# Two routers of a transformer kernel: position tables in 16 bits with the tile innermost, code products from written-out 16-bit tables

## The chip, the cores and the metric

The kernel runs on one core of one Trainium2 chip. The metric is the device time of one launch in microseconds (us). Five engines work side by side from queues of their own: PE (TensorE, matrix products; PEld is its loading of weights), DVE (VectorE), ACT (ScalarE), POOL (GpSimd) and SP (SyncE, which here only issues DMA).

## The reference, cut to what matters

2048 tokens of 256 numbers pass through two layers. Each layer has a mixing part (attention in layer 0) and then a layer of eight experts that a router chooses. Only the routers are touched here:

```python
# layer 0: the best expert of each token, at most C = 320 tokens per expert
top1 = jnp.argmax(logits, axis=-1)
mask = jax.nn.one_hot(top1, E, dtype=jnp.int32)
ranks = jnp.cumsum(mask, axis=0) - 1
mask = mask * (ranks < C).astype(jnp.int32)
...
dispatch = jnp.einsum('tec,th->ech', sec_mask, tokens)
# layer 1: the two best experts of each token, no limit
vals, idx = jax.lax.top_k(scores, TOP_K)
...
coef = (jax.nn.one_hot(sel, gate_w.shape[0], dtype=x.dtype) * mult[..., None]).sum(axis=1)
out = jnp.einsum('te,eth->th', coef, y)
```

## The kernel before

The 2048 tokens are 16 tiles (NT) of 128 (P), one token of a tile on each partition. The program is a row of phases, each a block of five instruction streams, one per engine. A barrier of all engines ends each block; its place in the profile is the branch line behind the phase (L983 behind router 0, L1436 behind router 1). The phases are `phase_front` (attention of layer 0), `phase_router0`, `phase_experts0`, `phase_mix`, `phase_router1`, `phase_experts1`. Within a stream the order is that of the code; engines wait for each other by semaphores.

Both routers do the same. PE turns the normalized rows, multiplies by the gate and turns the logits back. DVE, one small step after another, finds the best expert of each token, the rank of the token within its expert, and from it a slot: a block number and a position in the block of 0 to 127. Then the map token to slot has to be turned round into slot to token:

- `at_blk` (L1210, L1646) is 1 where the token's block is b. NS0 = 24 blocks in router 0; NB = 39 blocks and two choices j per token in router 1.
- `code` or `code_of` is `at_blk` times the number of the partition, plus one (`tok1`, L1211, L1649), and `at_blk` times the number of the tile (`iota_hi`, L1212, L1650).
- `at_pos` (L1215, two halves of 8 tiles; L1653, one instruction for each choice) is 1 where the token's position is p: every position p of a token is compared with the numbers 0 to 127 in `iota_pos`.
- PE multiplies `at_pos` of a tile, as weights, with the tile's codes and sums over the tiles (L1099, L1541). The sum at (p, b) is the token in slot p of block b.

DVE reads it out (`tok0`, L1234; `tok_of`, L1664), and POOL gathers the rows of the first blocks from DRAM by an indirect DMA (L974, L944) as the last thing of the block. In `phase_experts1`, `at_pos` of router 1 is used once more, on 32 weight loads, to carry the weights of the tokens to their slots (L2257, shown as e_w). In router 0 SP issues bulk loads all the time (weights of expert 1, and those of the mixing part, L952 and L960).

The number tables are written by POOL at the start of each router's block, one `iota` after another (`numbers`, L1252 and L1669), in 32-bit floats: router 0 has eight and DVE waits for them at its `wait_ge(iota_ready, 8)`; router 1 has seven and DVE waits for six of them. At that time DVE runs the start of its own stream: `memset` and copy of `gT` (L1592, L1593 in router 1), `normal_rows` (L140: 128x256 each, four for a quarter of the tokens), and then `turned` (L1147, L1582), half of the copy of the turned rows, on which PE's product of logits waits (L1051, L1492).

Two helpers set the shape of an operand:

```python
def bcast(ap, n):        # [p, w] read as [p, n, w]: the whole row again and again
    return ap.unsqueeze(1).to_broadcast([ap.shape[0], n, ap.shape[1]])
def last_bcast(ap, n):   # [p, w] read as [p, w, n]: each element n times in a row
    return ap.unsqueeze(2).to_broadcast([ap.shape[0], ap.shape[1], n])
```

Of the kernel before, what the change touches and what calls it, by code (L numbers as in the profile page):

```python
# [978 lines left out]
def phase_router0(nc, k, a, sem):  # L979
# [3 lines left out]
    with ctx:  # L983
        def sb(name, shape, dt=FP):
            return ctx.enter_context(nc.sbuf_tensor("r0_" + name, shape, dt))
# [13 lines left out]
        logits, best, diff = sb("logits", [P, NT, E]), sb("best", [P, NT]), sb("diff", [P, NT, E])  # L999
        desc, iota_pos, iota_b = sb("desc", [P, E]), sb("iota_pos", [P, P]), sb("iota_b", [P, NS0])  # L1000
        iota_hi, iota_empty, tok1 = sb("iota_hi", [P, NT]), sb("iota_empty", [P, E, NST]), sb("tok1", [P, 1])
        upper = sb("upper", [P, 1])
# [3 lines left out]
        tot, run, rank = sb("tot", [P, E, NT]), sb("run", [P, E, NT]), sb("rank", [P, NT, E])  # L1006
        sel, hi2, pos, blk = sb("sel", [P, NT]), sb("hi2", [P, NT]), sb("pos", [P, NT]), sb("blk", [P, NT])
        full, sel_i = sb("full", [P, NT]), sb("sel_i", [P, NT], mybir.dt.int32)
        at_pos, at_blk = sb("at_pos", [P, NT, P], BF), sb("at_blk", [P, NT, NS0], BF)
        code = sb("code", [P, NT, 5, NS0], BF)  # L1010
# [33 lines left out]
        def _(pe):  # L1044
# [53 lines left out]
            def invert(out, c0, c1, i):  # L1098
                return nc.tensor.matmul(out, at_pos[:, i, :], code[:, i, c0:c1, :].rearrange("p c b -> p (c b)"),  # L1099
                                        start=(i == 0), stop=(i == NT - 1))  # L1100
# [39 lines left out]
        def _(dve):  # L1140
# [70 lines left out]
            step(ts(code[:, :, 0, :], at_blk[:, :, :], tok1[:, 0:1], None, ALU.mult))  # L1211
            step(tt(code[:, :, 1, :], at_blk[:, :, :], last_bcast(iota_hi[:, :], NS0), ALU.mult))  # L1212
            for half in range(2):
                some = slice(NT // 2 * half, NT // 2 * (half + 1))
                tt(at_pos[:, some, :], bcast(iota_pos[:, :], NT // 2), last_bcast(pos[:, some], P),  # L1215
                   ALU.is_equal).then_inc(pos_ready, 1)
# [32 lines left out]
        @block.gpsimd  # L1249
        def _(pool):  # L1250
            def numbers(out, pattern, base, each):
                nc.gpsimd.iota(out, pattern=pattern, base=base, channel_multiplier=each,  # L1252
                               allow_small_or_imprecise_dtypes=True).then_inc(iota_ready, 1)

            numbers(desc[:, :], [[-1, E]], E, 0)
            numbers(iota_b[:, :], [[1, NS0]], 0, 0)
            numbers(iota_pos[:, :], [[1, P]], 0, 0)
            numbers(iota_hi[:, :], [[1, NT]], 0, 0)
            numbers(tok1[:, :], [[0, 1]], 1, 1)
            for r in range(NST - 1):  # L1260
# [172 lines left out]
def phase_router1(nc, k, a, sem):  # L1433

    ctx = ExitStack()
    with ctx:  # L1436
# [15 lines left out]
        best, pri, rest = sb("best", [P, NT]), sb("pri", [P, NT, E]), sb("rest", [P, NT, E])  # L1452
        desc, iota_b, iota_pos = sb("desc", [P, E]), sb("iota_b", [P, NB]), sb("iota_pos", [P, BLK])
        iota_end, iota_hi, tok1 = sb("iota_end", [P, NB]), sb("iota_hi", [P, 2 * NT]), sb("tok1", [P, 1])
        cont, chosen = sb("cont", [P, E, NT]), sb("chosen", [P, NT, E], BF)
# [3 lines left out]
        pick, slot = sb("pick", [P, 2, NT, E]), sb("slot", [P, 2 * NT])  # L1459
        slot_i, blk_of, pos = sb("slot_i", [P, 2 * NT], mybir.dt.int32), sb("blk_of", [P, 2 * NT]), sb("pos", [P, 2 * NT])  # L1460
        code_of = sb("code_of", [P, 2, NT, 2, NB], BF)
        cmp_b, blk_e = sb("cmp_b", [P, NB, E]), sb("blk_e", [P, NB])
        inv = sb("inv", [P, NB])
# [21 lines left out]
        def _(pe):  # L1485
# [52 lines left out]
            for j in range(2):  # L1538
                pe.wait_ge(pos_ready[j], 1)
                for i in range(NT):  # L1540
                    last = nc.tensor.matmul(pinv[:, 0:2 * NB], k.at_pos[:, j, i, :],  # L1541
                                            code_of[:, j, i, :, :].rearrange("p s b -> p (s b)"),
                                            start=(j == 0 and i == 0), stop=(j == 1 and i == NT - 1))
# [31 lines left out]
        def _(dve):  # L1575
# [62 lines left out]
            for j in range(2):  # L1638
# [10 lines left out]
            step(ts(code_of[:, :, :, 0, :].rearrange(flat4), at_blk[:, :, :, :].rearrange(flat4), tok1[:, 0:1], None, ALU.mult))  # L1649
            tt(code_of[:, :, :, 1, :].rearrange(flat4), at_blk[:, :, :, :].rearrange(flat4), last_bcast(iota_hi[:, :], NB),  # L1650
               ALU.mult).then_inc(code_ready, 1)
            for j in range(2):
                tt(k.at_pos[:, j, :, :], bcast(iota_pos[:, :], NT), last_bcast(pos[:, NT * j:NT * (j + 1)], BLK),  # L1653
                   ALU.is_equal).then_inc(pos_ready[j], 1)
# [11 lines left out]
        @block.gpsimd  # L1666
        def _(pool):
            def numbers(out, pattern, base, each):
                nc.gpsimd.iota(out, pattern=pattern, base=base, channel_multiplier=each,  # L1669
                               allow_small_or_imprecise_dtypes=True).then_inc(iota_ready, 1)  # L1670

            numbers(desc[:, :], [[-1, E]], E, 0)
            numbers(iota_b[:, :], [[1, NB]], 0, 0)
            numbers(iota_pos[:, :], [[1, BLK]], 0, 0)
            numbers(iota_end[:, :], [[BLK, NB]], 0, 0)
            numbers(iota_hi[:, :].rearrange("p (j i) -> p j i", j=2), [[0, 2], [1, NT]], 0, 0)
            numbers(tok1[:, :], [[0, 1]], 1, 1)
# [479 lines left out]
def phase_experts1(nc, k, a, sem, out):  # L2157
# [4 lines left out]
    with ctx:  # L2162
# [43 lines left out]
        def _(pe):  # L2206
# [46 lines left out]
            def slot_weights():  # L2253
                pe.wait_ge(wcode_ready, 1)
                for n in range(2 * NT):
                    j, i = divmod(n, NT)
                    last = nc.tensor.matmul(pw[:, :, :].rearrange("p n b -> p (n b)"), k.at_pos[:, j, i, :],  # L2257
                                            k.wcode[:, j, i, :, :].rearrange("p n b -> p (n b)"),
                                            start=(n == 0), stop=(n == 2 * NT - 1))
                last.then_inc(w_done, 1)  # L2260
# [337 lines left out]
```

## Time and profile before

| | us |
|---|---|
| median of 3 runs | 1077.09 (1077.02 to 1078.98) |
| the profiled execution | 1082.88 |
| its span in the profile | 1081.2 |
| PE busy | 965.0 (89%) |
| DVE busy | 634.9 (59%) |
| ACT busy | 525.2 (49%) |
| POOL busy | 291.7 (27%) |

The profile is that of one execution, 1082.88 us long; instructions and waits are read from its span of 1081.2 us. Router 0 lies from 507.4 to 546.0 us of it, the experts of layer 0 up to 710, the mixing part up to 803.4, router 1 from 803.4 to 839.8, the experts of layer 1 behind it. The profile names a buffer by its first letters and without numbers (`r_at_pos`, `r_code`; both routers' are `r_...`; `k_at_pos` is that of router 1; `r_plT` and `e_w` are banks of PSUM; `k_hT` at L2363 is the table of weight codes). A line number is that of the kernel printed above.

### The profile page before, as it was taken

To read this page: it belongs to the slowest core of one execution; us is meant where nothing else is said; L and a number is where in the kernel's file an instruction comes from. 1 tells how busy PE (TensorE), PEld (TensorE's weight loads), DVE (VectorE), ACT (ScalarE), POOL (GpSimd) and SP (SyncE) were. 2 spreads that over 40 slices of the span, in tenths; PEclk is the share of its full clock that TensorE was granted. 3 is DMA by queue.
4 is the path that set the end of the run, shared out by engine and by line. 5 is a ranking of instruction groups with operands and counts; after the bars stand their busy time and mean duration, and the time that the engine had idled before them with its cause. 6 is when DMAs were issued, how large, how long until landed. Compare 5 with 4: busy or idle time off the path is not lost. (4 is left out here: it accounts for less than half of the span.)

```text
span 1081.2 us, 24756 instructions
## 1 busy us (share of the span) xinstructions
PE 965.0 (89%) x9947; PEld 635.2 (59%) x9951; DVE 634.9 (59%) x1667; ACT 525.2 (49%) x825; POOL 291.7 (27%) x345
## 2 busy tenths in 40 slices
PE   7788899999999999997579999967885899999993
PEld 4333335444444444444257777755664799999993
DVE  5568999999898979675610000088677533333331
ACT  3432567777875786763222213176443444444440
POOL 2100420110111111132024342225450155544541
PEclk9978999999999999998879999989997899999997
DMA  5880000000000000011935668230560033332224
GB/s 188 171 181 15 2 2 2 3 3 2 3 3 2 3 2 2 2 4 64 371 103 146 215 178 269 44 85 1 176 214 1 25 53 51 47 49 49 47 41 96
DMA packets 63279, 78.87 MB, mean 73 GB/s; under 512 B 12096, under 2 KB 54976, under 8 KB 62736
## 3 DMA queue, kind: packets, MB, share of 16 engines
q1 hardware_dynamic: 50688, 61.54, 19.0%
q0 software_dynamic: 11968, 15.47, 8.6%
q8 instruction: 68, 1.11, 0.4%
q10 hardware_dynamic: 528, 0.52, 0.1%
q14 instruction: 27, 0.22, 0.1%
HBM read 58.12 MB, written 21.36 MB: 74 GB/s over the span
## 5 line engine op out<-in xcount | busy, mean ns | idle before, releaser
L622 ACT ACTIVATE k_prob<-f_s 128x1024 f32<-128x1024 f32 (+3 forms) x320 | 270.1, 896 | 121.5 <-PE f_s L460 120.9
L682 DVE TENSOR_REDUCE k_mpart<-f_r 128x1 f32<-128x512 f32 x384 | 250.5, 685 | 34.5 <-PE f_r L403 32.2
L403 PE MATMUL f_r<-k_ks,k_qs 112*32 112x512 bf16 (+3 forms) x2560 | 211.8, 357 | 20.7 <-DMA k_qs<-q_dram 8.1
L460 PE MATMUL f_s<-k_qs,k_ks 114*32 114x512 bf16 (+3 forms) x2560 | 174.9, 350 | 1.9 <-ACT k_prob L622 1.3
L882 POOL TENSOR_SCALAR_AFFINE_SELECT k_prob<-k_prob 128x256 f32<-128x256 f32 x128 | 51.2, 406 | 383.9 <-ACT k_prob L622 382.7
L403 PEld LDWEIGHTS f_r<-k_ks,k_qs 112*32 112x32 bf16 x2560 | 70.1, 95 | 137.4 <-DVE k_mpart L682 56.7
L476 PE MATMUL f_o<-k_prob,k_vaug 128*32 128x512 f32 (+3 forms) x1280 | 146.6, 531 | 1.5 <-POOL k_prob L882 1.4
L679 DVE CUSTOM_DVE_ANT_0 k_unread<-f_r,k_causal 128x128 bf16<-128x128 f32 (+3 forms) x256 | 121.0, 484 | 18.7 <-PE f_r L403 17.7
L460 PEld LDWEIGHTS f_s<-k_qs,k_ks 114*32 114x32 bf16 x2560 | 65.3, 97 | 78.5 <-issue 27.5
L2321 DVE TENSOR_TENSOR mid<-silu_g,e_u 128x512 f32<-128x512 f32 x39 | 26.8, 688 | 112.7 <-PE e_u L2222 111.7
L1406 DVE SCALAR_TENSOR_TENSOR outr<-p_o,k_w,k_mod 128x256 f32<-128x256 f32 x16 | 7.7, 484 | 131.1 <-PE p_o L1347 131.1
L2222 PE MATMUL e_g<-xT,k_rot_t 128*128 128x128 f32 x624 | 77.9, 279 | 2.9 <-ACT xT L147 2.9
L2222 PEld LDWEIGHTS e_g<-xT,k_rot_t 128*128 128x128 f32 x624 | 77.2, 195 | 5.4 <-ACT xT L147 3.5
L2409 POOL DMA_INDIRECT sum<-y,k_row_of x39 | 62.3, 1598 | 65.1 <-DVE y L2332 51.8
L1378 ACT ACTIVATE mid<-p_h 128x320 f32<-128x320 f32 x64 | 28.0, 437 | 104.1 <-PE p_h L1335 104.1
L2222 PE MATMUL e_u<-xT,k_rot_t 128*128 128x128 f32 x624 | 77.1, 277 | 0.0
L1335 PE MATMUL p_h<-rowsT,k_w1T 128*128 128x320 f32 x256 | 73.8, 448 | 1.2 <-ACT rowsT L147 1.2
L2222 PEld LDWEIGHTS e_u<-xT,k_rot_t 128*128 128x128 f32 x624 | 74.0, 195 | 0.0
L2233 PE MATMUL e_y<-k_w1T,mid 128*128 x312 | 73.6, 379 | 0.0
L944 POOL DMA_INDIRECT k_xb<-h_rows,k_tok_of x39 | 44.8, 1148 | 91.9 <-PE e_x L2216 54.5
L1424 POOL DMA_INDIRECT sum<-outr,k_row x24 | 37.8, 1576 | 93.4 <-DVE outr L1406 91.6
L1335 PEld LDWEIGHTS p_h<-rowsT,k_w1T 128*128 128x128 f32 x256 | 49.6, 196 | 22.8 <-issue 3.2
(403 smaller groups left out, 1264.9 us busy)
## 6 DMA issues: line engine op xcount, KB each, us to landing
k_w1T<-in_L_ffn_w_dram SPq DMA_DIRECT2D x18, 512.0 KB, 9.8
k_w1T<-in_L_ffn_wi_dram SPq DMA_DIRECT2D x8, 1024.0 KB, 5.9
k_w1T<-in_L_ffn_wo_dram SPq DMA_DIRECT2D x8, 1024.0 KB, 9.4
k_qs<-q_dram SPq DMA_DIRECT2D x6, 768.0 KB, 9.4
h_rows<-k_h SPq DMA_DIRECT2D x8, 512.0 KB, 6.6
sum<-k_x SPq DMA_DIRECT2D x8, 512.0 KB, 6.7
q_dram<-k_room SPq DMA_DIRECT2D x12, 256.0 KB, 9.2
k_rot_t<-in_L_ffn_w_dram SPq DMA_DIRECT2D x6, 512.0 KB, 4.9
```

The source lines that it names most:

```text
L403: last = nc.tensor.matmul(dst[32 * j:32 * (j + 1), :], qs[0:KROWS, c, GH * g + hs, q0:q0 + 32], ks[0:KROWS, QC * ck:QC * ck + w], start=Tr ...
L460: last = nc.tensor.matmul(sc[h % 2][32 * j:32 * (j + 1), i, off:QC], ks[0:KALL, k0:k0 + 32], qs[0:KALL, c, GH * g + 2 * pair + i, off:QC], ...
L476: last = nc.tensor.matmul(ot[32 * j:32 * (j + 1), off:QC], vaug[:, kt, :], prob[:, u % 2, j, off:QC], start=(kt == 0), stop=(kt == TQ * (c ...
L622: nc.scalar.activation(prob[:, u % 2, 2 * pair:2 * pair + 2, off:QC], sc[h % 2][:, :, off:QC], ACT.Exp, scale=HD ** -0.5).then_inc(e_done, 1)
L679: nc.vector.tensor_tensor_reduce(unread[:, r % RING, 0:w], bank(r)[:, 0:w], causal[:, QC - w:QC], 1.0, NEG, ALU.add, ALU.max, mpart[:, s % ...
L682: nc.vector.reduce_max(mpart[:, s % 2, hs, t, ck:ck + 1], bank(r)[:, 0:w], AX.X).then_inc(ring_used[r % RING], 1)
L882: nc.gpsimd.affine_select(out=block_, in_=block_, compare_op=ALU.is_ge, fill=0.0, base=0, pattern=[[0, 2], [1, P]], channel_multiplier=-1) ...
L944: nc.gpsimd.indirect_dma_start(out=k.xb[:, b % 2, :], out_offset=None, in_=k.h_rows, in_offset=bass.IndirectOffsetOnAxis(ap=k.tok_of[:, b: ...
L1335: last = nc.tensor.matmul(ph[n % 2][:, 0:CAP], wi[:, s, t, P * n:P * (n + 1)], rowsT[:, s, t, :], start=(t == 0), stop=(t == KH - 1))
L2222: last = nc.tensor.matmul(out[:, P * c:P * (c + 1)], w[:, s, F1 * t + P * c:F1 * t + P * (c + 1)], xT[:, s, t, :], start=(t == 0), stop=(t ...
L2233: last = nc.tensor.matmul(py[s][:, :], m[:, s, P * c:P * (c + 1)], k.w1T[:, e, 2, D * c:D * (c + 1)], start=(c == 0), stop=(c == FT - 1))
L2409: nc.gpsimd.indirect_dma_start(out=k.sum1, out_offset=bass.IndirectOffsetOnAxis(ap=k.row_of[:, b:b + 1], axis=0), in_=y[:, s, :], in_offse ...
```

## The change

Three things change in each router, and nothing in the order of any stream: each engine has as many instructions as before, in the same order.

- `at_pos` is stored as (position, tile) in place of (tile, position), so that the 16 tiles of a position are next to each other. It is computed from a table `all_pos` of the same shape, which holds the position 16 times over, and from `pos`, both in 16 bits. `pos` is now read as a row of 8 or 16 elements again and again.
- The product with the tile's number takes a table `hi_of` in the full shape of `at_blk`, in 16 bits, in place of `iota_hi`. The codes keep their layout.
- PE reads `at_pos` of a tile as weights with a step of 16 elements (32 bytes) between columns, in place of a step of one: 32 weight loads in router 0, 32 in router 1 and 32 in the experts of layer 1.

POOL writes the two tables: in router 0, 2048 elements in place of 128 and 384 in place of 16; in router 1, 2048 in place of 128 and 1248 in place of 32; all in 16 bits in place of 32.

```diff
# phase_router0
+        all_pos, hi_of = sb("all_pos", [P, P, NT], BF), sb("hi_of", [P, NT, NS0], BF)
...
-                return nc.tensor.matmul(out, at_pos[:, i, :], code[:, i, c0:c1, :].rearrange("p c b -> p (c b)"),
+                return nc.tensor.matmul(out, at_pos[:, :, i], code[:, i, c0:c1, :].rearrange("p c b -> p (c b)"),
...
-            step(tt(code[:, :, 1, :], at_blk[:, :, :], last_bcast(iota_hi[:, :], NS0), ALU.mult))
+            step(tt(code[:, :, 1, :], at_blk[:, :, :], hi_of[:, :, :], ALU.mult))
...
-                tt(at_pos[:, some, :], bcast(iota_pos[:, :], NT // 2), last_bcast(pos[:, some], P),
+                tt(at_pos[:, :, some], all_pos[:, :, some], bcast(pos[:, some], P),
                    ALU.is_equal).then_inc(pos_ready, 1)
...
-            numbers(iota_pos[:, :], [[1, P]], 0, 0)
-            numbers(iota_hi[:, :], [[1, NT]], 0, 0)
+            numbers(all_pos[:, :, :], [[1, P], [0, NT]], 0, 0)
+            numbers(hi_of[:, :, :], [[1, NT], [0, NS0]], 0, 0)
# phase_router1
-                    last = nc.tensor.matmul(pinv[:, 0:2 * NB], k.at_pos[:, j, i, :],
+                    last = nc.tensor.matmul(pinv[:, 0:2 * NB], k.at_pos[:, j, :, i],
...
-            tt(code_of[:, :, :, 1, :].rearrange(flat4), at_blk[:, :, :, :].rearrange(flat4), last_bcast(iota_hi[:, :], NB),
+            tt(code_of[:, :, :, 1, :].rearrange(flat4), at_blk[:, :, :, :].rearrange(flat4), hi_of[:, :, :],
                ALU.mult).then_inc(code_ready, 1)
...
-                tt(k.at_pos[:, j, :, :], bcast(iota_pos[:, :], NT), last_bcast(pos[:, NT * j:NT * (j + 1)], BLK),
+                tt(k.at_pos[:, j, :, :], all_pos[:, :, :], bcast(pos[:, NT * j:NT * (j + 1)], BLK),
                    ALU.is_equal).then_inc(pos_ready[j], 1)
...
-            numbers(iota_pos[:, :], [[1, BLK]], 0, 0)
+            numbers(all_pos[:, :, :], [[1, BLK], [0, NT]], 0, 0)
             numbers(iota_end[:, :], [[BLK, NB]], 0, 0)
-            numbers(iota_hi[:, :].rearrange("p (j i) -> p j i", j=2), [[0, 2], [1, NT]], 0, 0)
+            numbers(hi_of[:, :, :].rearrange("p (j i) b -> p j i b", j=2), [[0, 2], [1, NT], [0, NB]], 0, 0)
# phase_experts1
-                    last = nc.tensor.matmul(pw[:, :, :].rearrange("p n b -> p (n b)"), k.at_pos[:, j, i, :],
+                    last = nc.tensor.matmul(pw[:, :, :].rearrange("p n b -> p (n b)"), k.at_pos[:, j, :, i],
```

## Rows read from the trace of the kernel before

**Rows 1.** The chain that ended last, shares of the span by line.

```profile
by line: PE e_g L2222 6.7%; PE e_u L2222 6.5%; PE e_y L2233 6.1%; PE e_x L2216 0.8%; DMA sum<-y,k_row_of 0.3%; PE e_w L2257 0.2%; issue 0.2%; POOL sum L2409 0.1%; ACT xT L147 0.1%; ACTq L2291 0.1%; DVE y L2332 0.0%; ACT k_rot_t L2292 0.0%; 
```

**Rows 2.** DVE late in router 0, in order of time (start, duration, in us).

```profile
531.05 2.36 DVE L1215 TENSOR_TENSOR r_at_pos<-r_iota_pos,r_pos 128x1024 bf16<-128x1024 f32 x2
533.94 1.50 DVE L1221 TENSOR_TENSOR r_code<-r_at_blk,r_w_part 128x384 bf16<-128x384 bf16 x3
536.27 0.18 DVE L1234 CAST k_tok<-r_row 128x24 uint32<-128x24 f32 x1
```

**Rows 3.** Router 0's end on POOL, SP and PE, and its gathers' time to landing.

```profile
540.18 0.91 POOL L974 DMA_INDIRECT k_rows<-h_rows,k_tok  x1 [0.30 <-issue]
DMA to landing us min/median/max: 5.4/5.4/6.1
542.57 0.90 SPq L960 DMA_DIRECT2D k_bq<-in_L_attn_b_in_dram  x1
546.05 1.87 PE L1323 MATMUL p_t<-k_ident,k_rows 128*128 128x128 f32 x6 [9.41 <-PEq L983]
```

**Rows 4.** DVE at the end of router 1.

```profile
829.27 4.49 DVE L1653 TENSOR_TENSOR k_at_pos<-r_iota_pos,r_pos 128x2048 bf16<-128x2048 f32 x2
835.14 0.20 DVE L1662 COPY r_inv<-r_plT 128x39 f32<-128x39 f32 x1
835.60 0.18 DVE L1664 TENSOR_SCALAR k_tok_of<-k_slot 128x39 uint32<-128x39 f32 x1
```

**Rows 5.** Router 1's end on PE and POOL; a stretch: busy by engine, granted clock 0.78.

```profile
833.81 1.22 PE L1541 MATMUL r_plT<-r_code_of,k_at_pos 128*128 128x78 bf16 x16 [0.91 <-DVE k_at_pos L1653]
836.64 1.07 POOL L944 DMA_INDIRECT k_xb<-h_rows,k_tok_of  x1 [32.23 <-DVE k_tok_of L1664]
831.00:831.50 0.50, 0.00 (x0) 0.00 (x0) 0.50 (x2) 0.00 (x0) 0.00 (x0) 0.78 0.00 0
```

**Rows 6.** DVE groups by line and shape (busy us, mean ns of one).

```profile
L2363 DVE TENSOR_TENSOR k_hT<-k_at_blk,e_w_hi 128x1248 bf16<-128x1248 bf16 x3 | 4.2, 1454 | 0.0
L1649 DVE TENSOR_SCALAR r_code_of<-k_at_blk,r_tok 128x1248 bf16<-128x1248 bf16 x1 | 0.6, 553 | 0.0
```

**Rows 7.** The start of router 1 on POOL, DVE and PE.

```profile
803.68 0.29 DVE L1593 COPY r_gT<-k_g_in 128x16 f32<-128x16 f32 x1
803.70 0.23 POOL L1669 IOTA r_iota_pos<- 128x128 f32 x1
805.11 0.80 DVE L1582 TENSOR_SCALAR k_hT<-r_tp,k_modcol_b 128x512 f32<-128x512 f32 x1
806.62 1.41 PE L1492 MATMUL r_plT<-k_hT,r_gT 128*32 128x512 f32 x4
```

**Rows 8.** The start of router 0, and the same copy of gT without POOL beside it.

```profile
507.62 1.40 DVE L140 TENSOR_SCALAR k_h<-k_x,k_mv,k_rstd 128x256 f32<-128x256 f32 x4
509.07 3.25 PE L178 MATMUL r_tp<-k_ident,k_h 128*128 128x128 f32 x14 [0.57 <-DVE k_h L140]
510.30 0.16 DVE L1164 COPY r_gT<-k_g_in 128x16 f32<-128x16 f32 x1
```

**Rows 9.** POOL and DVE side by side in the attention; all runs of L663.

```profile
479.04 0.41 POOL L882 TENSOR_SCALAR_AFFINE_SELECT k_prob<-k_prob 128x256 f32<-128x256 f32 x1 [0.51 <-ACT k_prob L622]
479.15 0.44 DVE L663 TENSOR_SCALAR k_gate_sgn<-k_mod 128x256 f32<-128x256 f32 x1
L663 DVE TENSOR_SCALAR k_gate_sgn<-k_mod x2: 289/364/440, 116.7 to 479.1; 128x256 f32<-128x256 f32 x2
```

**Rows 10.** POOL: a short iota in time, and a 16-bit output by line and shape.

```profile
803.47 0.14 POOL L1669 IOTA r_desc<- 128x8 f32 x1 [0.52 <-POOLq L1689]
L831 POOL TENSOR_SCALAR k_minus<-k_ident 128x128 bf16<-128x128 f32 x1 | 0.6, 585 | 0.4 <-DMA k_bo<-in_L_attn_bo_dram 0.4
```

**Rows 11.** Part of the longest chain in the experts of layer 1, in order of time.

```profile
856.00 1.78 PE e_g L2222 x16
861.52 1.73 PE e_w L2257 x32
```

More of the change, by code:

```diff
@@ L999, in phase_router0 @@
         logits, best, diff = sb("logits", [P, NT, E]), sb("best", [P, NT]), sb("diff", [P, NT, E])
-        desc, iota_pos, iota_b = sb("desc", [P, E]), sb("iota_pos", [P, P]), sb("iota_b", [P, NS0])
-        iota_hi, iota_empty, tok1 = sb("iota_hi", [P, NT]), sb("iota_empty", [P, E, NST]), sb("tok1", [P, 1])
+        desc, iota_b = sb("desc", [P, E]), sb("iota_b", [P, NS0])
+        iota_empty, tok1 = sb("iota_empty", [P, E, NST]), sb("tok1", [P, 1])
         upper = sb("upper", [P, 1])
@@ L1006, in phase_router0 @@
         tot, run, rank = sb("tot", [P, E, NT]), sb("run", [P, E, NT]), sb("rank", [P, NT, E])
-        sel, hi2, pos, blk = sb("sel", [P, NT]), sb("hi2", [P, NT]), sb("pos", [P, NT]), sb("blk", [P, NT])
+        sel, hi2, pos, blk = sb("sel", [P, NT]), sb("hi2", [P, NT]), sb("pos", [P, NT], BF), sb("blk", [P, NT])
         full, sel_i = sb("full", [P, NT]), sb("sel_i", [P, NT], mybir.dt.int32)
-        at_pos, at_blk = sb("at_pos", [P, NT, P], BF), sb("at_blk", [P, NT, NS0], BF)
+        at_pos, at_blk = sb("at_pos", [P, P, NT], BF), sb("at_blk", [P, NT, NS0], BF)
+        all_pos, hi_of = sb("all_pos", [P, P, NT], BF), sb("hi_of", [P, NT, NS0], BF)
         code = sb("code", [P, NT, 5, NS0], BF)
@@ L1452, in phase_router1 @@
         best, pri, rest = sb("best", [P, NT]), sb("pri", [P, NT, E]), sb("rest", [P, NT, E])
-        desc, iota_b, iota_pos = sb("desc", [P, E]), sb("iota_b", [P, NB]), sb("iota_pos", [P, BLK])
-        iota_end, iota_hi, tok1 = sb("iota_end", [P, NB]), sb("iota_hi", [P, 2 * NT]), sb("tok1", [P, 1])
+        desc, iota_b = sb("desc", [P, E]), sb("iota_b", [P, NB])
+        iota_end, tok1 = sb("iota_end", [P, NB]), sb("tok1", [P, 1])
         cont, chosen = sb("cont", [P, E, NT]), sb("chosen", [P, NT, E], BF)
@@ L1459, in phase_router1 @@
         pick, slot = sb("pick", [P, 2, NT, E]), sb("slot", [P, 2 * NT])
-        slot_i, blk_of, pos = sb("slot_i", [P, 2 * NT], mybir.dt.int32), sb("blk_of", [P, 2 * NT]), sb("pos", [P, 2 * NT])
+        slot_i, blk_of, pos = sb("slot_i", [P, 2 * NT], mybir.dt.int32), sb("blk_of", [P, 2 * NT]), sb("pos", [P, 2 * NT], BF)
         code_of = sb("code_of", [P, 2, NT, 2, NB], BF)
+        all_pos, hi_of = sb("all_pos", [P, BLK, NT], BF), sb("hi_of", [P, 2 * NT, NB], BF)
         cmp_b, blk_e = sb("cmp_b", [P, NB, E]), sb("blk_e", [P, NB])
@@ L2536, in build @@
         with experts1:
-            k.at_pos = sbuf(experts1, "at_pos", [P, 2, NT, BLK], BF)
+            k.at_pos = sbuf(experts1, "at_pos", [P, 2, BLK, NT], BF)
             k.hT1 = sbuf(experts1, "hT1", [P, 2 * KH * QC])
```

## The prediction

> **What bounds the kernel now.** I read the longest chain first: it ends in the experts of layer 1, in PE's products back to back [rows 1]. Then the two routers in order of time, engine by engine: there nobody is busy throughout, and PE and POOL wait for DVE's small steps. So a router's end is set by one chain, and what that gains or loses moves everything behind it.
>
> Router 0 [rows 2, 3]: DVE works without a pause up to `k_tok`, written at 536.45; then POOL gathers, the third gather starts at 540.18 and lands 5.4 us later, at about 545.6; PE goes on at 546.05 behind the barrier. SP's last issue ends at 543.47, so the gathers end last and SP some 2 us ahead of them. Router 1 [rows 4, 5]: DVE writes `k_tok_of` at 835.78, POOL gathers from 836.64, and the block ends. Just before, two things meet: PE's last product ends at 835.03, and DVE, busy until then, reads it at 835.14. At the start of both routers DVE's L140 leads to PE's next step: in router 0 PE waits for it (0.57 us), in router 1 `turned` (805.11 to 805.91) is done 0.7 us before PE can start the logits at 806.62 [rows 7, 8].
>
> **Part 1: DVE's tables.** Price of a two-input operation: 1.18 us for 1024 elements (2.36 for two) [rows 2], 2.25 for 2048 (4.49 for two) [rows 4]: 1.04 ns an element and 0.11 us fixed. Two 16-bit inputs alone don't help: L2363 has them, one repeated along the innermost dimension, and takes 1454 ns for 1248, the full price. A one-input operation on as many 16-bit elements takes 553 ns [rows 6], so 16-bit elements can be taken several at a time. For a two-input one the trace has no such row. Bounds: nothing gained, and half the elements' time. I take the half, since now every operand is 16-bit with neighbours next to each other. Then each operation loses half its elements' time.
>
> - Router 0: two halves of `at_pos`, each 0.53 less; code product, 192 elements' time of 384, 0.20 less. Sum 1.26.
> - Router 1: two `at_pos`, each 1024 x 1.04, 1.06 less; code product, 624 elements' time of 1248 (priced by L2363, its like), 0.65 less. Sum 2.77.
>
> The Trainium skill ("VectorE: DVE Perf Modes", What auto-detection actually checks) says that a two-input operation runs two elements a cycle if every tensor is 16-bit with step one. By it the sums are these; without it they would be zero. No row here shows it.
>
> All of this is on the chain, if PE keeps up. In router 1 the first `at_pos` is ready at about 829.8 in place of 831.5, PE needs for 16 pairs of load and product 1.22 us even at the low clock [rows 5], the second is ready at 831.0, so PE ends by 832.3, when DVE is ready to read too (835.1 - 2.77). In router 0 PE has the three code products of L1221 as cover (1.50 us). The clock falls from 2.4 to 1.2 GHz about 831.3 (0.78 granted over 831.0 to 831.5, [rows 5]), so the first 16 pairs run no slower than now.
>
> **Part 2: PE's weight loads, step 32 bytes.** Now a pair takes 76 ns in router 1 (1.22 by 16, low clock) and 54 ns in the experts (1.73 by 32) [rows 5, 11], with products of 78 and 117 columns, so a load hides behind a product. No weight load of this kernel has a step now. Lower bound: no change. Upper bound, by the slowest row of pairs: a 32-bit load and product, 111 ns (1.78 by 16) [rows 11], and 222 at half the clock. That would cost 32 x 0.057 = 1.8 us at L2257, and in router 1: 13 pairs by 831.3 and 19 x 0.222 after it, end at 835.5 in place of 832.3, 3.2 us. Sum 5.0. I take no change: a load has a whole product's time to hide in.
>
> The Trainium skill ("Advanced Engine Details and Errata", SBUF Cachelines) speaks against the change: lines are 16 bytes, and accesses that each go to another line pay. Every column is now on a line of its own. The page has no price; by it the truth lies between the two bounds.
>
> **Part 3: POOL's tables.** Price of an iota: 0.14 us for 8 elements [rows 10], 0.23 for 128 [rows 7], so about 0.8 ns an element. At that price `all_pos` takes 0.14 + 2048 x 0.8 = 1.78 us in place of 0.23, `hi_of` 1.14 in router 1 and 0.45 in router 0. DVE waits for the tables only behind the fourth `turned`; in router 1 the first is at 805.11, and each further one waits for PE, while the tables would be done at 807.1 (803.70 + 1.78 + 1.14 and four small ones). So nothing by that wait. But DVE is held off while POOL writes or reads, and the rows show it within 0.01 us. L663 takes 289 ns alone and 440 beside POOL's L882: it ends at 479.59, and POOL ended at 479.45; what is left, 0.14 us, is the latter half of its own time [rows 9]. The copy of `gT` takes 0.16 alone and 0.29 beside the iotas, and ends at 803.97, 0.04 behind the iota of 128 elements [rows 7, 8]. DVE's L140, four in 1.40, is such an operation too. With the iota of 2048 elements in that place:
>
> - Router 1: `gT` ends 0.04 behind 803.70 + 1.78, that is 1.55 late. Then `hi_of` comes between two of the L140s and holds DVE for about 1 us more. `turned` is 2.5 late, 0.7 of it is slack, so the logits start 1.8 late. From there PE works without a pause; nothing is won back.
> - Router 0: L140 starts at 507.62 [rows 8], while POOL is at that iota: 1.5 late, and `hi_of` adds 0.4. PE waits for L140 there without slack: 1.9 late.
>
> Lower bound of this part: nothing, if a long iota lets DVE in between its writes. Upper bound: see the second rival.
>
> **The sum**, in the profiled execution: router 0 -1.26 + 1.9 = +0.6; router 1 -2.77 + 1.8 = -1.0; weight loads 0. Together -0.3 to -0.4. The gathers of router 0 land later by 0.6, behind bulk traffic that is by then thinner, so perhaps less. Its span is 1081.2 and its time 1082.88, 5.8 above the median of 1077.09; the routers' steps are the same in both, so I take the difference off the median: 1076.8.
>
> **Rivals.**
>
> 1. POOL's long iotas don't hold DVE: router 0 -1.26, router 1 -2.77, sum -4.0, 1073.1. For it: only short iotas are in the trace, and a long one may let DVE in between. Against: [rows 7, 9]. SP's own end (543.47) leaves room for router 0's part. Chance 0.25.
> 2. Slower: a 16-bit iota costs more an element than a 32-bit one. POOL's one plain 16-bit output from 32-bit numbers, L831, takes 585 ns for 128 elements, 3.5 ns each [rows 10]. DVE is held for it in full: 5728 elements in both routers (2432 and 3296) times the excess over 0.8. At 2.0 ns this is +6.9 and the time 1083.7; at 3.5 ns +15.5, 1092. It decides from 1.25 ns on (+2.5). For it: the row. Against: it multiplies as well, and an iota has nothing to read. Chance 0.22.
> 3. Slower: the strided loads at their upper bound, +5.0 - 0.4, 1081.7; at half the way the time is over the bound of no change. Chance 0.07.
> 4. The change doesn't do what it says, DVE's operations keep their 2284 ns: nothing gained, part 3 paid in full, +3.7, 1080.8. Chance 0.04.
>
> **How the numbers follow.** My forecast has 0.42; its own range is 1075.3 to 1078.8, by the parts of `hi_of` (1 us in all), of the clock at the logits (up to 1 us either way) and of a small excess in the loads. A measurement can tell about 0.2% (2.15 us) from no change, so faster means below 1074.9: rival 1 nearly whole (0.23) and the forecast's edge (0.05), 0.28. Slower means above 1079.2: most of rivals 2 to 4 (0.30) and an edge of 0.02, 0.32. The same: 0.40. The range must take in rival 1 (1073.1, with 0.6 below) and the small end of rivals 2 and 3: 1072.5 to 1084.0; above it lies the greater part of rival 2, below it 0.04.
>
> **What would show it.** `at_pos` of 2048 at about 1220 ns and of 1024 at 690, codes at 808 and 358 (part 1). L1541 at 16 pairs in 1.2 us or less, L2257 still at 1.73 (part 2). The iota of `all_pos` at 1.8 us; the copy of `gT` in router 1 at 1.8 us in place of 0.29, ending with that iota; the first logits of router 1 some 5.0 behind the block's start in place of 3.2 (part 3). I am wrong if `gT` and L140 keep their times beside the iota (then rival 1), or if the iota takes several us (rival 2).

## The result, and the profile after

| | kernel before | changed kernel |
|---|---|---|
| median of the runs, us | 1080.3 (20 runs) | 1081.64 (20 runs) |
| ratio to the kernel before | | 1.0026, 95% interval 1.0015 to 1.0038 |
| profiled execution, us | 1082.88 | 1086.18 |
| its span, us | 1081.2 | 1084.5 |

The change costs 0.26%, some 2.8 us. The two medians differ by only 1.3 us and the two means by 3.2: the 20 runs of the changed kernel lie in two groups, 12 at 1080.3 to 1082.1 us and 8 at 1084.3 to 1086.7, and the profiled execution is one of the upper group. The forecast was 0.3 to 0.4 us faster, within what can't be told from no change; the loss is outside its own range (to 1078.8 against 1077.09, that is +1.7) and inside the wide one (to 1084.0, that is +6.9).

Line numbers in the changed kernel are one higher in router 0 and two higher from router 1 on. The start of router 0, in order of time (start, duration in us):

```profile
507.49 2.49 POOL L1253 IOTA r_all_pos<- 128x2048 bf16 x1
507.51 3.82 DVE L140 TENSOR_SCALAR k_h<-k_x,k_mv,k_rstd 128x256 f32<-128x256 f32 x4
509.92 0.63 POOL L1253 IOTA r_hi_of<- 128x384 bf16 x1
511.38 0.47 PE L178 MATMUL r_tp<-k_ident,k_h 128*128 128x128 f32 x1 [2.99 <-DVE k_h L140]
```

Four L140 take 3.82 us in place of 1.40 [rows 8]: DVE stands still until POOL's iota ends at 509.98, and PE starts its transposes 2.4 us late. Router 0 late:

```profile
533.15 0.36 DVE L1213 TENSOR_TENSOR r_code<-r_at_blk,r_hi_of 128x384 bf16<-128x384 bf16 x1
533.55 1.29 DVE L1216 TENSOR_TENSOR r_at_pos<-r_all_pos,r_pos 128x1024 bf16<-128x1024 bf16 x2
534.36 1.22 PE L1100 MATMUL r_plT<-r_code,r_at_pos 128*128 128x48 bf16 x16
537.71 0.18 DVE L1235 CAST k_tok<-r_row 128x24 uint32<-128x24 f32 x1
```

Two `at_pos` in 1.29 us in place of 2.36 [rows 2]: the tables' gain is there in full. The start of router 1:

```profile
805.35 0.14 POOL L1671 IOTA r_desc<- 128x8 f32 x1 [0.52 <-POOLq L1691]
805.56 2.53 DVE L1595 COPY r_gT<-k_g_in 128x16 f32<-128x16 f32 x1
805.59 2.47 POOL L1671 IOTA r_all_pos<- 128x2048 bf16 x1
805.65 5.13 DVE L140 TENSOR_SCALAR k_h<-k_x,k_mv,k_rstd 128x256 f32<-128x256 f32 x4
808.15 1.83 POOL L1671 IOTA r_hi_of<- 128x1248 bf16 x1
811.64 1.07 PE L1494 MATMUL r_plT<-k_hT,r_gT 128*32 128x512 f32 x2 [2.62 <-DVE k_hT L1584]
```

The copy of 16 elements takes 2.53 us where it took 0.29 [rows 7], and ends with the iota. L140 is then held by `hi_of` as well. And the end of router 1:

```profile
835.20 0.81 DVE L1652 TENSOR_TENSOR r_code_of<-k_at_blk,r_hi_of 128x1248 bf16<-128x1248 bf16 x1
835.92 2.35 DVE L1655 TENSOR_TENSOR k_at_pos<-r_all_pos,r_pos 128x2048 bf16<-128x2048 bf16 x2
837.29 2.30 PE L1543 MATMUL r_plT<-r_code_of,k_at_pos 128*128 128x78 bf16 x32 [2.49 <-DVE k_at_pos L1655]
841.20 1.07 POOL L944 DMA_INDIRECT k_xb<-h_rows,k_tok_of  x1 [30.98 <-DVE k_tok_of L1666]
```

Here 2.35 stands for 4.49 [rows 4]. Since the phases start at other times in each execution, what counts is the distance from each router's own start (POOL's first iota), in us:

| from the block's start to | before | changed |
|---|---|---|
| router 0: first transpose on PE | 1.67 | 4.09 |
| DVE's `at_blk` | 22.10 | 24.92 |
| `k_tok` | 28.87 | 30.42 |
| PE goes on in the experts | 38.65 | 40.00 |
| router 1: first logits on PE | 3.15 | 6.29 |
| DVE's `chosen` | 16.48 | 21.91 |
| `at_blk` | 22.34 | 27.77 |
| `cmp_b`, behind both `at_pos` | 30.20 | 32.84 |
| gather | 33.17 | 35.85 |

Both routers together are 4.0 us longer (1.35 and 2.68). A large loss at the start is partly paid back by the tables. In router 1 the logits start 3.1 late and `chosen` is 5.4 late, so 2.3 more are lost over the logits. The granted clock there, from the block's start in stretches of 3 us (length, then busy PE, weight loads, DVE, ACT and POOL, then the clock as a share of 2.4 GHz, the DMA share and GB/s); the first 9 us of the kernel before:

```profile
803.47:806.47 3.00, 2.98 (x16) 2.82 (x16) 2.35 (x7) 1.37 (x2) 0.93 (x7) 0.58 0.98 323
806.47:809.47 3.00, 3.00 (x20) 1.46 (x20) 1.33 (x4) 1.53 (x3) 0.00 (x0) 0.85 0.96 319
809.47:812.47 3.00, 3.00 (x20) 1.36 (x20) 1.44 (x4) 1.35 (x2) 0.00 (x0) 1.00 0.00 0
```

and the first 12 of the changed one:

```profile
805.35:808.35 3.00, 2.98 (x14) 3.00 (x15) 2.90 (x4) 0.92 (x2) 3.00 (x5) 0.50 0.89 295
808.35:811.35 3.00, 0.67 (x4) 0.27 (x2) 3.00 (x4) 0.64 (x1) 1.86 (x3) 0.50 0.00 0
811.35:814.35 3.00, 2.71 (x8) 1.08 (x9) 1.07 (x4) 0.58 (x1) 0.00 (x0) 0.50 0.89 300
814.35:817.35 3.00, 3.00 (x14) 1.40 (x12) 0.81 (x1) 0.78 (x1) 0.00 (x0) 0.50 0.15 50
```

Before, PE works on and is back at 2.4 GHz some 4 us behind the block's start. Now it pauses for 2.6 us, and stays at 1.2 GHz until 12 us behind the start. In this profile the clock had fallen 1.6 us ahead of the block. In a second one of the changed kernel (e10_after) it fell 1.4 us behind the start (0.5 in the kernel before), and `chosen` came at 21.70 all the same.

### The profile page after: what moved, and what is told of

The parts are those of the page before. It is cut to its first block and busy times, and to the rows that moved or that the text cites. A ratio compares the mean times of both kernels' runs of the same rounds, so it can differ in the third digit from the quotient of the medians.

```text
span 1084.5 us, 24759 instructions
## 1 busy us (share of the span) xinstructions
PE 972.3 (90%) x9950; PEld 636.4 (59%) x9951; DVE 636.6 (59%) x1667; ACT 525.5 (48%) x825; POOL 298.1 (27%) x345
## 5 line engine op out<-in xcount | busy, mean ns | idle before, releaser
L882 POOL TENSOR_SCALAR_AFFINE_SELECT k_prob<-k_prob 128x256 f32<-128x256 f32 x128 | 51.3, 407 | 383.8 <-ACT k_prob L622 382.6
```

What stands on the lines that cost most here:

```text
L882: nc.gpsimd.affine_select(out=block_, in_=block_, compare_op=ALU.is_ge, fill=0.0, base=0, pattern=[[0, 2], [1, P]], channel_multiplier=-1) ...
```

## The experiments

Theory H: POOL's long iotas hold DVE at both routers' starts, and the clock behind PE's pause adds to the price in router 1. Rival R: the loss lies in the strided weight loads.

**e1_late_both.** The long tables are written behind the fourth `turned`, and DVE waits for them just ahead of the code product:

```
-            numbers(all_pos[:, :, :], [[1, P], [0, NT]], 0, 0)
-            numbers(hi_of[:, :, :], [[1, NT], [0, NS0]], 0, 0)
...
+            pool.wait_ge(hT2_ready, NC)
+            numbers(all_pos[:, :, :], [[1, P], [0, NT]], 0, 0, table_ready)
+            numbers(hi_of[:, :, :], [[1, NT], [0, NS0]], 0, 0, table_ready)
...
+            dve.wait_ge(table_ready, 2)
```

> The changed kernel, with POOL writing all_pos and hi_of of both routers only behind the fourth turned of DVE (DVE waits for them just ahead of the code product), so that they lie beside no L140 and no copy of gT. Theory H (POOL's long iotas hold DVE at the routers' start, and the logits behind that pause of PE run at a lower clock): L140 four in 1.4 us again, PE's first transpose of router 0 at 1.6 us behind the block's start (4.1 in the changed kernel), first logits of router 1 at 3.2 us behind it (6.3), the clock over the logits at 0.8 (0.50), and both routers keep the gain of the tables (1.3 and 2.8 us). Time 3.0 to 4.0 us under the kernel before, ratio about 0.9965. Rival R (the loss is elsewhere, in the strided weight loads or what follows the routers): no nearer to the kernel before than the changed kernel is, ratio 1.002 or more. A third case: DVE's operations on the logits are held instead by the late tables (their 290 ns grow), and the gain is smaller by up to 3.1 us in router 0 and 4.3 in router 1.

Measured: ratio 0.996 (0.9944 to 0.9976), some 4 us under the kernel before. The first transpose comes at 1.65 us, the logits of router 1 at 2.69; `k_tok` at 27.68 and the gather at 30.42, 1.2 and 2.75 under before. POOL and DVE where the tables now lie in router 1, from its second profile (e11_late_again, below):

```profile
810.46 2.49 POOL L1676 IOTA r_all_pos<- 128x2048 bf16 x1 [8.14 <-DVE k_hT L1588]
810.56 0.22 DVE L1596 TENSOR_TENSOR k_lg<-k_lg,r_plog 128x64 f32<-128x64 f32 x1
812.91 1.85 POOL L1676 IOTA r_hi_of<- 128x1248 bf16 x1
813.97 0.23 DVE L1595 COPY k_lg<-r_plog 128x64 f32<-128x64 f32 x1 [3.19 <-PE r_plog L1507]
814.23 0.22 DVE L1596 TENSOR_TENSOR k_lg<-k_lg,r_plog 128x64 f32<-128x64 f32 x1
814.49 0.29 DVE L1613 TENSOR_REDUCE k_top<-k_lg 128x16 f32<-128x128 f32 x1
```

The iotas are as long as in the changed kernel, and beside them the sums of the logits (one input in PSUM) keep their 0.22 us and the reduction its 0.29. A copy passes too: L1595 reads `r_plog`, a bank of PSUM, and takes 0.23 us beside `hi_of`, where the copy of `gT`, from SBUF to SBUF (the memory in which the kernel's buffers lie), had waited for the end of the iota. The third case that I had named did not come. Theory H holds as to the hold of DVE, and R falls: the strided loads are still there. The part of the clock is tested by e9_filled.

**e2_hold_only.** The kernel before, with the two long tables of each router written early and read by nobody (DVE's wait for the tables counts them, as in the changed kernel):

```
+            numbers(all_pos[:, :, :], [[1, P], [0, NT]], 0, 0)
+            numbers(hi_of[:, :, :], [[1, NT], [0, NS0]], 0, 0)
             numbers(iota_pos[:, :], [[1, P]], 0, 0)
```

> The kernel before, where POOL also writes the two long 16-bit tables of each router at the place where the changed kernel writes them; nobody reads them, all else is as before. Theory H: the hold alone costs what the changed kernel lost plus what its tables gained: router 0 +2.7, router 1 +5.4 us, time 7 to 8 us over the kernel before, ratio 1.0065 to 1.0075; the copy of gT takes 2.5 us and the first L140 2.6 us. Rival C (router 1's logits ran slow in the changed kernel's profile by chance of the clock, not because of PE's pause): router 1 +3.1 only, ratio about 1.0055. Rival R (the hold is hidden): ratio 1.000 to 1.002.

Measured: 1.006 (1.0039 to 1.008), some 6.5 us. First transpose at 4.09, first logits of router 1 at 6.31, as in the changed kernel. The blocks are 2.8 and 4.3 us longer, 7.1 in all; `chosen` is 4.3 late and not 5.4, as the clock came back to 1.0 for 3 us in between. The time is a little under the 7 to 8 us that I had expected, and its interval takes in Rival C (1.0055) as well: this run shows the hold, and leaves the part of the clock to e9_filled. The hold costs 6.5 us by the runs, of which the tables pay 4.0 back by the blocks.

**e3_layout_only.** The kernel before, `at_pos` with the tile innermost, computed from the old 32-bit tables:

```
-                tt(at_pos[:, some, :], bcast(iota_pos[:, :], NT // 2), last_bcast(pos[:, some], P),
+                tt(at_pos[:, :, some].rearrange("p q i -> p i q"), bcast(iota_pos[:, :], NT // 2), last_bcast(pos[:, some], P),
```

> The kernel before, with at_pos alone laid out as in the changed kernel (tile innermost): DVE computes it from the same 32-bit small tables as before, writing at a step of 32 bytes, and PE reads its weights at a step of 32 bytes. No long iota. Prices the strided loads alone. By the changed kernel's profile (32 pairs at the weights in 2.15 us where they took 1.73; 16 pairs of router 0 in 1.22 where the second 16 took 1.14): a load takes some 70 ns, the whole +0.4 to +0.9 us, ratio 1.0005, the same if DVE's strided writes stay at 1.04 ns an element (4.49 us for two). If strided loads were what made the changed kernel slow: +2.8 us or more, ratio 1.0026. Should DVE's strided writes be dearer, this shows in its two operations on at_pos and is taken off.

Measured: 1.0141 (1.012 to 1.0162), a miss. Its time says nothing on the loads, as DVE's writes became dear: by the rows the four operations take 19.2 us more in all, which is more than the 15.2 that the runs lost, so that nothing for the loads is left when it is taken off (groups by line: busy us, mean ns):

```profile
L1653 DVE TENSOR_TENSOR k_at_pos<-r_iota_pos,r_pos 128x2048 bf16<-128x2048 f32 x2 | 17.3, 8842 | 0.0
L1215 DVE TENSOR_TENSOR r_at_pos<-r_iota_pos,r_pos 128x1024 bf16<-128x1024 f32 x2 | 8.8, 4560 | 0.0
```

A 16-bit element written at a step of 32 bytes takes 4.3 ns, where in order it took 1.1. Its 32 weight loads at the weights of the experts have a median of 152 ns, as in the changed kernel, against 98 in the kernel before. That priced the loads (see e7_pairs).

**e4_short.** The changed kernel, `all_pos` with each position twice, `hi_of` short likewise, repeated by a step of 0:

```
+                tt(at_pos[:, :, some].rearrange("p q (r s) -> p q r s", s=2), again(all_pos[:, :, :], NT // 4),
+                   bcast(pos[:, some], P).rearrange("p q (r s) -> p q r s", s=2), ALU.is_equal)
```

> The changed kernel with short tables in the same early place: all_pos holds each position twice (256 elements), hi_of each number twice in router 0 (32) and 13 times in router 1 (416); DVE repeats them by a step of 0 in a middle dimension, with neighbours in 16 bits next to each other innermost as in the changed kernel. Theory H: POOL's iotas take 0.45 us for all_pos and 0.15 and 0.65 for hi_of in place of 2.5, 0.6 and 1.8; the hold is nearly that of the kernel before, and if DVE keeps the short operations (690 and 1175 ns) the time is 3 to 4 us under the kernel before, ratio 0.997. If DVE's price needs the table written out in full, its operations are back at 1.2 and 2.25 us and the time is that of the kernel before or 0.5 over it, ratio 1.0005. Rival R (loss elsewhere): ratio 1.002.

Measured: 0.9966 (0.9953 to 0.9978). DVE keeps the short prices (688 and 1218 ns). But the iota of 256 elements takes 1.56 us, not 0.45, and holds L140 so long that PE starts at 2.92; router 1 pauses for 1.5 us, and its gather comes at 34.46, 1.3 later than before. By its blocks it is only 0.2 us from the kernel before (-1.05 and +1.29); the runs say -3.7 of 1081. What is between the two I can't name: the part behind router 1 alone varies by 2.6 us over the profiles (below). The time is the one that I had expected, but by luck: the short iotas, on which that expectation rested, did not come.

**e5_late_r0 and e6_late_r1.** The edit of e1_late_both in one router alone.

> The changed kernel with router 0's long tables alone written behind the fourth turned; router 1 as in the changed kernel. Theory H, by the two routers' blocks: router 0 is 1.2 us shorter than in the kernel before (PE goes on at 37.4 us behind the block's start, 38.7 before, 40.0 in the changed kernel), router 1 is 2.7 longer (gather at 35.9, before 33.2). Against the kernel before +1.5 to +2 us, ratio 1.0015. If the routers are not independent (router 1's clock hangs on when router 0 ended), router 1 comes out otherwise than 35.9.

> The changed kernel with router 1's long tables alone written late; router 0 as in the changed kernel. Theory H: router 0 as in the changed kernel (+1.3 us), router 1 2.7 us shorter than in the kernel before (gather at 30.4 us behind the block's start). Against the kernel before -1.0 to -1.5 us, ratio 0.999; this and the last one together should add up to the changed kernel (+2.8) and the one with both late (-4.4).

Measured: 1.0004 (0.9987 to 1.0021) and 0.9999 (0.9981 to 1.0017). The intervals, 3.7 and 3.9 us wide, take in what was expected and are too wide for the split; the blocks show it. With router 0 late: PE goes on at 37.58, gather of router 1 at 35.53 (35.85 in the changed kernel). With router 1 late: 38.85 and 30.42. So each router keeps its own loss. Router 0 with early tables was 1.35 longer than before in the changed kernel, and 0.2 here; its first transpose came at 4.09 in both. How much of that hold reaches the end hangs on the clock over the transposes and logits (0.79 here and 0.50 there, 6 to 8 us behind the start).

**e7_pairs.** Late tables, and `at_pos` in pairs of tiles, so that PE's weights have a step of 4 bytes:

```
-        at_pos, at_blk = sb("at_pos", [P, P, NT], BF), sb("at_blk", [P, NT, NS0], BF)
+        at_pos, at_blk = sb("at_pos", [P, NT // 2, P, 2], BF), sb("at_blk", [P, NT, NS0], BF)
...
+                return nc.tensor.matmul(out, at_pos[:, i // 2, :, i % 2], code[:, i, c0:c1, :].rearrange("p c b -> p (c b)"),
```

> Both tables late, and at_pos laid out in pairs of tiles: for each pair of tiles 128 positions, the two tiles next to each other innermost. PE's weights then have a step of 4 bytes in place of 32, all_pos has 256 elements, repeated by a step of 0 in the outermost dimension; DVE writes at_pos contiguously. Theory S (a load pays for its step): with four columns in each 16 bytes a load takes the 96 to 99 ns of the contiguous layout, or little more, in place of 152; the 32 pairs at the weights of the experts take 1.73 to 1.9 us (2.15), router 1 is 0.1 to 0.4 shorter; time 0.4 to 0.8 us under the one with late tables alone, ratio 0.9955 to the kernel before. Rival: every step other than 2 bytes costs the same: loads stay at 152 ns and 2.15 us. DVE's operations stay at 690 and 1218 ns, since the short tables showed the short price with two neighbours innermost.

Measured: 0.9968 (0.995 to 0.9985). The weight loads of e_w by line (busy us, mean ns), in the kernel before:

```profile
L2257 PEld LDWEIGHTS e_w<-k_hT,k_at_pos 128*128 128x128 bf16 x32 | 1.8, 98 | 0.1
```

In the changed kernel:

```profile
L2259 PEld LDWEIGHTS e_w<-k_hT,k_at_pos 128*128 128x128 bf16 x32 | 2.2, 152 | 0.1
```

In this one:

```profile
L2272 PEld LDWEIGHTS e_w<-k_hT,k_at_pos 128*128 128x128 bf16 x32 | 1.8, 98 | 0.1
```

The load pays for its step: 54 ns more at 32 bytes, nothing at 4. On the path this is small. From the first of the 32 pairs to the products behind them (863.09, 867.26, 859.60) it is 1.73, 2.00 and 1.73 us. PE in order of time in the kernel before:

```profile
861.36 1.89 PE L2257 MATMUL e_w<-k_hT,k_at_pos 128*128 128x117 bf16 x32
863.09 1.11 PE L2222 MATMUL e_g<-xT,k_rot_t 128*128 128x128 f32 x8
```

In the changed kernel:

```profile
865.26 2.15 PE L2259 MATMUL e_w<-k_hT,k_at_pos 128*128 128x117 bf16 x32
867.26 2.01 PE L2224 MATMUL e_g<-xT,k_rot_t 128*128 128x128 f32 x16
```

And in this one:

```profile
857.87 1.90 PE L2272 MATMUL e_w<-k_hT,k_at_pos 128*128 128x117 bf16 x32
859.60 2.00 PE L2237 MATMUL e_g<-xT,k_rot_t 128*128 128x128 f32 x16
```

0.27 us, not the 0.42 that my expectations took from two unlike views. In router 1 the gather comes at 30.33 us here and at 30.42 in e1_late_both.

**e8_iota_forms.** The kernel before with eight further iotas of POOL in router 0:

```
+            again(0, try32[:, :], [[1, NT * P]])
+            again(1, try16[:, :], [[1, NT * P]])
+            again(2, try16[:, :].rearrange("p (q i) -> p q i", i=NT), [[1, P], [0, NT]])
+            again(3, try32[:, :].rearrange("p (q i) -> p q i", i=NT), [[1, P], [0, NT]])
...
+            again(5, try16[:, :].rearrange("p (q i) -> p i q", i=NT), [[0, NT], [1, P]])
+            again(6, try16[:, 0:2 * P].rearrange("p (q s) -> p q s", s=2), [[1, P], [0, 2]])
```

> The kernel before with eight further iotas of POOL in router 0, behind the fourth turned, where POOL waits anyway; nobody reads them. In order: 2048 elements as one run in 32 bits, the same in 16 bits; 128 runs of 16 equal numbers in 16 bits, and in 32 bits; 16 runs of 128 in 16 bits written contiguously, and written with the tile innermost; 128 runs of 2 in 16 bits; one run of 128 in 16 bits. Theory T (16 bits cost more an element, 1.15 ns against 0.8): 1.8, 2.5, 2.5, 1.8, 2.5, 2.5 us, and so on. Rival N (POOL pays for each run, some 10 ns by the short tables: 256 elements in 128 runs took 1.5 us, 2048 in as many 2.5): 1.2 to 1.6 us for one run in either type, 2.5 for 128 runs of 16 in either type, 1.3 to 1.8 for 16 runs of 128, 1.5 for 128 runs of 2, 0.2 for one run of 128.

Its one run took 1090.89 us. Measured, numbers 0 to 3, 5 and 6 on POOL in order of time:

```profile
518.93 1.84 POOL L1269 IOTA r_try<- 128x2048 f32 x1 [10.34 <-DVE k_w1T L1149]
520.83 1.84 POOL L1269 IOTA r_try<- 128x2048 bf16 x1
522.74 2.48 POOL L1269 IOTA r_try<- 128x2048 bf16 x1
525.28 2.46 POOL L1269 IOTA r_try<- 128x2048 f32 x1
529.79 8.73 POOL L1269 IOTA r_try<- 128x2048 bf16 x1
538.60 1.54 POOL L1269 IOTA r_try<- 128x256 bf16 x1
```

Number 4, 16 runs of 128 written in order, took 1.91 us, and number 7, one run of 128, 0.24. 16 and 32 bits cost the same, so theory T falls. N holds in kind (POOL pays for each run) but not in size: it had 1.2 to 1.6 us for one run of 2048 and some 10 ns a run. One run of 2048 takes 0.83 ns an element ((1.84 - 0.14) / 2048), 128 runs of 16 take 5 ns a run more (0.64 / 128), 128 runs of 2 take 11 ns each, elements and all (1.40 / 128). Writing with the tile innermost takes 4.3 ns an element here as on DVE. Meanwhile on DVE:

```profile
528.27 0.29 DVE L1196 COPY r_tot<-r_prt 128x128 f32<-128x128 f32 x1 [0.29 <-DVE r_w_left L1193]
529.78 0.29 DVE L1202 TENSOR_TENSOR r_rank<-r_rank,r_one_hot 128x128 f32<-128x128 f32 x1
530.11 0.29 DVE L1203 TENSOR_REDUCE r_sel<-r_rank 128x16 f32<-128x128 f32 x1
530.43 8.13 DVE L1205 CAST r_sel_i<-r_sel 128x16 int32<-128x16 f32 x1
538.60 1.57 DVE L1206 TENSOR_SCALAR r_sel_i<-r_sel_i 128x16 int32<-128x16 int32 x1
```

A two-input operation and a reduction pass beside the iota at their own 0.29 us; a cast of 16 elements waits 8 us for its end at 538.52, and the one-input operation behind it for the end of the next. A copy of 128 elements out of PSUM (`r_prt`, beside number 4) takes 0.29 and waits for nothing, as in e1_late_both. So those held are copies, casts and one-input operations with both ends in SBUF. The Trainium skill ("SBUF — State Buffer", Who interferes with whom) names copies, casts and `tensor_scalar` as operations that can take the ports shared with POOL, and reductions as never held on trn2; the trace agrees. It has operations with two inputs in SBUF contend with POOL's reads and not with its writes; the iota's rows show no input, and the two-input operation passes.

**e9_filled.** The changed kernel, with 14 idle transposes where PE pauses in router 1:

```
                 if q == 1:
+                    for n in range(14):
+                        nc.tensor.transpose(prt[:, 0, :], k.ident[:, :], k.ident[:, :])
                     pe.wait_ge(gate_ready, 1)
```

> The changed kernel with 14 idle transposes of the identity on PE in router 1, behind the eighth pair of transposes and ahead of the wait for gT, where PE pauses in the changed kernel; their result is never read. The hold of DVE stays as it is. Theory P (the second part of router 1's loss is the clock: PE's pause keeps TensorE at 1.2 GHz for 8 us more): PE works on through the hold, the granted clock is back at 1.0 some 4 to 5 us behind the block's start as in the kernel before (11 to 12 in the changed kernel), the first logits still start at 6.3 us, but `chosen` comes at 19.2 to 20.0 (21.9 in the changed kernel, 16.5 before): router 1 is 2 us shorter than in the changed kernel, the time 2 us under it. Rival (the clock falls and returns by itself, not by PE's pause): the clock returns at 11 us all the same, the idle transposes take 0.23 us each, hold the logits to 7.3, and router 1 is 1 us longer than in the changed kernel.

Measured: 1.0005 (0.9989 to 1.0021), where the changed kernel beside it had 1.0027. The logits start at 6.29 us, as in the changed kernel, but `chosen` comes at 19.27 (21.91) and the gather at 33.18 (35.85). Router 1's first 9 us in stretches of 3, columns as above:

```profile
800.69:803.69 3.00, 2.98 (x19) 3.00 (x20) 2.90 (x4) 1.56 (x2) 3.00 (x5) 0.68 0.89 294
803.69:806.69 3.00, 2.15 (x13) 1.91 (x11) 3.00 (x4) 0.00 (x0) 1.86 (x3) 0.75 0.00 0
806.69:809.69 3.00, 2.71 (x18) 1.50 (x20) 1.60 (x5) 1.36 (x2) 0.00 (x0) 1.00 0.89 300
```

The clock is back before the logits begin. DVE is held just as long, and 2.6 us are won by work that is thrown away: that part of the loss was the clock behind PE's pause. Theory P holds. The two intervals (this one, and e10_after's below) overlap, but the means of the 12 runs each are 2.7 us apart, with a standard error of 0.9, and agree with the blocks.

**e10_after, e11_late_again, e12_pairs_again.** The three kernels once more, beside each other.

> The changed kernel itself once more, beside the others of this group, for a comparison on one chip. Expected by what the first comparison gave: 2.8 us over the kernel before, ratio 1.0026; router 0's block 1.3 us longer in its first profile, of which up to 1.1 hung on the clock over its logits (the kernel with router 1's tables late has the same router 0 and took 0.2 longer only); so between 0.2 and 1.4 here.

> The kernel with both routers' tables late once more, beside the one in pairs and the changed kernel. Expected: 4 us under the kernel before, ratio 0.996; 6 to 7 us under the changed kernel.

> The kernel in pairs of tiles with late tables once more. By the traces it should be 0.3 to 0.5 us under the one with late tables (the contiguous-like loads at 98 ns in place of 152, on the chain at the weights of the experts, e_w, and 0.1 in router 1), which a comparison of two medians can hardly show: 4.0 to 4.5 us under the kernel before. If its time is over the other's by more than 1.5 us, the pairs cost something that the rows do not show.

Measured: 1.0027 (1.001 to 1.0044), 0.996 (0.9942 to 0.9977), 0.9958 (0.9941 to 0.9976); medians 1084.27, 1077.09, 1076.73, and 1081.8 before. The changed kernel's blocks are 1.5 and 2.5 us longer than before. Late tables beat both kernels by 4 and 7 us. The pairs can't be told from them by time; their loads are again without the 54 ns. Their router 1 shows what the clock does by itself: it had fallen 1 us ahead of the block, `chosen` came at 17.54 and the gather at 31.45 (16.45 and 30.33 in e7_pairs, the same kernel). A single block is known to 1 us, no better.

## Why the prediction was wrong, by its steps

- **Part 1, DVE's tables: right.** Forecast 1.26 and 2.77; from `at_blk` to `k_tok` and to the gather the changed kernel takes 1.27 and 2.75 us less than before. `at_pos` took 686 and 1217 ns (forecast 690 and 1220), codes 360 and 809. By e11_late_again `k_tok` is 1.2 and the gather 2.7 us earlier.
- **Part 2, the strided loads: right to well under a microsecond.** Taken 0, measured 0.27 us at e_w. In both routers other work covers them but for 0.15 at most: from `at_blk` to `k_tok` it is 5.65 us in e1_late_both and 5.49 in e7_pairs, to the gather of router 1 8.06 and 8.03. The upper bound of 5.0 was far off. "A load has a whole product's time to hide in" was wrong: in router 0 16 pairs take 1.22 us, 76 ns each, where 8 took 0.37, 46 ns each, at the same granted clock of 1.00:

```profile
532.33 0.37 PE L1099 MATMUL r_plT<-r_code,r_at_pos 128*128 128x48 bf16 x8 [0.75 <-DVE r_at_pos L1215]
```

The rule on lines that the prediction cited from the Trainium skill ("Advanced Engine Details and Errata", SBUF Cachelines) agrees with this: a load costs more where every column has a line of its own (152 ns), and not where four share one (98 ns). No run here tries a step between the two.
- **Part 3, POOL's tables: right in kind, and this is the step that failed.** The held operations are the ones named: the copy of `gT` ends 0.04 us behind the iota, and the held L140 0.15 to 0.17 behind, as L663 did behind L882. Two terms of it were too small. *First, the iota's price.* `all_pos`, put at 1.78 us, measured 2.47 to 2.49, and `hi_of` 1.83 in place of 1.14. The 0.8 ns an element is right for one run (0.83); the table is written in 128 runs, and each costs extra. My two rows of iotas were both of one run. Router 0's hold was 2.4 in place of 1.9, router 1's logits 3.1 late in place of 1.8. *Second, the clock.* I put it into the own range as "up to 1 us either way"; it was 2.3 us in router 1 (5.43 late at `chosen` less 3.14 at the logits), and e9_filled gave it back. "From there PE works without a pause; nothing is won back" left out that more can be lost: I had not asked at which clock PE would start behind a pause of my own making. In router 0 this part was 0.4 (2.8 late at `at_blk`, 2.4 at the transposes).
- **The sum**, by the blocks of the first profile: router 0 +2.8 at `at_blk` less 1.27 (+1.35 where PE goes on; forecast +0.6), router 1 +5.43 less 2.79 (+2.68 at the gather; forecast -1.0), loads +0.3: 4.3 in place of -0.3. Of these 4.6 the iotas' price makes 1.8 (0.5 and 1.3), the clock 2.7 (0.4 and 2.3) and the loads 0.3, and 0.2 is won behind router 0's `k_tok`. The runs show 2.8 (1.6 to 4.1). The spans of the two profiles differ by 3.3: the stretch between the routers took 0.6 longer, and the part behind router 1, weight loads included, 243.3 in place of 244.6 us. Over all profiles this last part varies from 242.4 to 245.0 whatever the kernel, with 243.2 in the middle, so neither difference can be put down to the change.
- **The wide range** held by luck: its upper part stood there for Rivals 2 and 3, and neither came.
- **Rival 1** (no hold, 1073.1) fell as a forecast, but its time is what e1_late_both reached by moving the tables: 4.0 us gained by the blocks where 4.0 were worked out.
- **Rival 2** had the sign but not the mechanism: there is no dearer 16-bit iota. L831's 3.5 ns an element was no guide.
- **Rivals 3 and 4** fell: the loads cost 0.3 to 0.5 us and not 5.0, and DVE's operations took 1217 ns and not 2284.

## What to carry to other kernels

When a table is moved to another engine to be written once, price the writing where it will lie: which operation of the neighbour it holds, and who waits for that; in a stretch where DVE has no copy, cast or one-input operation from SBUF to SBUF the same 4 us of iota were free. When a change makes PE pause at the start of a stage, add to the pause what the products behind it lose until the clock is back: here 2.3 on top of 3.1 us. And take an iota's price from one with as many short runs as the new one has.

## What the runs showed of the hardware beyond that

- An iota costs by its runs (a run is a row of elements without an outer step of the pattern): 1.84 us for 2048 elements in one run, 2.48 in 128 runs, and 1.54 for an eighth of the elements in as many. 32 runs of 39 took 1.83 and 32 of 13 took 1.15, about 20 ns a run beyond the elements; 16 runs of 24 took 0.52 in e1_late_both, 4 ns a run beyond them, and 0.63 in the early place. Why the former are dearer was not tried.
- Writing 16-bit elements at a step of 32 bytes costs 4.3 ns an element on both DVE and POOL, some four and five times the price in order.
- The short price of DVE's two-input operations needs neighbours only in the innermost dimension, and two are enough: a middle dimension of step 0 leaves 1218 ns for 2048 elements as they are. A table of 128 positions by 16 need not be written out.
- The kernel before ran at 1076.1 to 1082.3 us in the first comparison. In the profiles router 0 starts either at 502.6 to 503.1 us or at 506.1 to 507.8, whatever the kernel: 3 to 5 us that arise ahead of everything that is changed here, so routers are best compared from their own start. Both profiles of the changed kernel (1086.18 and 1086.12 us) are of its upper group and start router 0 at 507.3 and 507.4; the lower group was not profiled.
